# A recurrence's rounds taken out of hardware loops, with constant semaphore waits in place of register waits

## The chip, the cores and the metric

The kernel runs on one core of a Trainium2 chip. The core has a matrix engine (TensorE, PE in the profile, its weight loads as PEld), VectorE (DVE), ScalarE (ACT), GpSimd (POOL) and SyncE (SP), which here only issues DMAs. Each engine works through its own list of instructions in order; they meet only in semaphores. The metric is the device time of one execution in microseconds, as the median of several runs.

## The reference, cut to what matters

`x` is 4 x 32 x 128 x 128 in fp32. A layer norm and a Fourier attention block are added to it, and the result, seen as 4 sequences of 4096 tokens of 128 channels, goes through a layer norm, a linear map with batch statistics, and a recurrence over the 4096 tokens, whose states are added to it:

```python
x = x + _L0_conv_ref(_ln_c(x), ...)
t = _to_tokens(x)
t = t + _L0_ffn_ref(_ln_t(t), L0_ffn_W, L0_ffn_V, L0_ffn_gamma, L0_ffn_beta)
...
    def step(yt, wx_t):
        yt = jax.nn.sigmoid(wx_t + yt @ Vt)
        return (yt, yt)
    y0 = jnp.zeros((B, H), dtype=Wx.dtype)
    _, ys = jax.lax.scan(step, y0, jnp.swapaxes(Wx, 0, 1))
```

`wx_t` is the normalized linear map of token t, `Vt` a 128 x 128 matrix.

## The kernel before

Up to about 520 us the kernel computes the attention block and the linear map; nothing of that is touched. The recurrence then is not run token by token. Each sequence is cut into 256 chunks of `STEPS` = 16 tokens, and all chunks advance together: one operation handles one step of the 256 chunks of one sequence, as a tile of 128 channels x 256. The four sequences are the `GR` = 4 groups.

A first sweep runs only the last 8 steps (`BURN`) of every chunk, from a guessed state. Its end states are handed to the next chunks as their starts, by `starts`, on VectorE: two copies for each group (L1385, of 128 x 224, and L1386, of 128 x 31). A second sweep then runs all 16 steps. `judge` compares the new end states with those that were used as starts. If they differ by more than `TOL`, a flag makes every engine repeat whole sweeps in a loop under `e.If`; in the profiled execution the flag is zero and no repeat is run.

A round is one step of all four groups. For each group it takes three operations on three engines: TensorE multiplies the state with `v_t` into PSUM (L588, called from `sweep` at L851 and L856; one such fp32 product is two weight loads and two matmul passes in the trace), VectorE adds the linear map's value to it (L1364, `add_z`), ScalarE takes the sigmoid and writes the new state (L990, L996), which is the input of the group's next product. The semaphores are `vy` (product done), `vy_wx` (addition done) and `state` (state written). Every engine has a `sweep` of its own; `recur` calls it on each.

In each `sweep` the first two rounds are written out, and their waits are on constants. The rest are turns of a loop (`Fori`, L852, L992, L1372), two rounds to a turn: 3 turns in the first sweep, 7 in the second. In a turn the wait's value depends on the loop's register `i`. Such a wait becomes an instruction of its own ahead of the operation; in the trace it stands as FUSED_REGOPS on the engine's sequencer (DVEq, ACTq, PEldq).

Beside this, GpSimd works on something that the recurrence does not need before `judge`: 32 additions of 128 x 512 (L581, fp32, two inputs in SBUF, `x1_g0`), one right behind the other. After the sweeps come the reading of the flag, 128 transposes on TensorE, 32 additions on VectorE (L1412) and 32 output DMAs.

Of the kernel before, what the change touches and what calls it, by code (L numbers as in the profile page):

```python
# [56 lines left out]
STEPS, BURN = 16, 8  # L57
# [78 lines left out]
def metaformer(nc, t, out):  # L136
# [4 lines left out]
    with ctx:  # L141
# [3 lines left out]
        def sem(name):  # L145
            return ctx.enter_context(nc.semaphore(name))
# [146 lines left out]
        def s(name):  # L293

            if name not in scn:
                scn[name] = len(scn)
                assert len(scn) <= 54
            return sc[:, scn[name]:scn[name] + 1]
# [16 lines left out]
        def S(name):  # L315

            if name not in sems:
                sems[name] = sem(name)
            return sems[name]
# [74 lines left out]
        def at(states, g, j):  # L394

            return states[:, :, bass.ds(j, 1), TB * g:TB * g + TB]

        def start(g):
            return start_a[:, :, TB * g:TB * g + TB].unsqueeze(2)

        def sums(g, dj):
            return PS[:, g + GR * dj, 0:Q * TB].rearrange("d (q j t) -> d q j t", q=Q, t=TB)

        def recur(e, sweep, starts=None, judge=None):


            sweep(0, 0, STEPS - BURN)
            if starts:
                starts(BURN)
            sweep(1, BURN, 0)  # L410
            rounds = BURN + STEPS
            if judge:
                judge(rounds)
            e.wait_ge(S("judged"), 1)
            again = e.value_load(FLAG[0:1, 0:1], min_val=0, max_val=1)
            with e.If(again > 0):
                with e.Fori(0, CHUNKS - 1) as i:
                    if starts:
                        starts(i * STEPS + rounds)
                    sweep(i + 2, i * STEPS + rounds, 0)  # L420
                e.wait_ge(S("state"), GR * (rounds + STEPS * (CHUNKS - 1)))
            e.wait_ge(S("state"), GR * rounds)

# [162 lines left out]
        def _(pe):  # L586
            def mm(o, l, rhs, start=True, stop=True, **k):
                return pe.matmul(o, l, rhs, start=start, stop=stop, **k)  # L588
# [144 lines left out]
            for g in range(32):  # L733
# [8 lines left out]
                if g >= 24:  # L742
                    n = g - 24
# [21 lines left out]
            for turn in range(0, G4 + LAG_P2, 4):  # L765
# [4 lines left out]
                for g in range(max(turn - LAG_P2, 0), min(turn - LAG_P2 + 4, G4)):  # L770
                    n, j = 4 * g // P2_T, 4 * g % P2_T
# [10 lines left out]
            for k, (bk, a) in X1_AT.items():  # L782
                n = 68 if 0 < k < 16 else 34
# [56 lines left out]
            pe.wait_ge(S("bn"), G4)  # L840
            mm(PS[:, 7, 511:512], v_t, ones[:, 0:1]).then_inc(S("v_sum_filled"), 1)

            def sweep(n, k0, j0):

                for dj in range(0 if j0 == 0 else 1, 2):
                    for g in range(GR):
                        if dj:
                            pe.wait_ge(S("state"), GR * k0 + g + 1)
                        else:
                            pe.wait_ge(S("start"), n * GR + (g + 1))  # L850
                        mm(sums(g, dj), v_t, at(y_s, g, j0) if dj else start(g)).then_inc(S("vy"), 1)  # L851
                with pe.Fori(1, (STEPS - j0) // 2) as i:  # L852
                    for dj in range(2):
                        for g in range(GR):
                            pe.wait_ge(S("state"), i * (2 * GR) + (GR * (k0 + dj) + g + 1 - GR))
                            mm(sums(g, dj), v_t, at(y_s, g, i * 2 + (j0 + dj - 1))).then_inc(S("vy"), 1)  # L856

            def judge(p):
                pe.wait_ge(S("gap"), 1)
                tr(PS[0:1, 0, 0:128], s("gap")).then_inc(S("gap_filled"), 1)  # L860

            recur(pe, sweep, None, judge)

            for g in range(G4):
# [9 lines left out]
        def _(act):  # L874
# [60 lines left out]
            for i in range(G4 + LAG_M2):  # L935
# [5 lines left out]
                if g >= 0 and (4 * g + 4) % P2_T == 0 or g == G4 - 1:  # L941
                    n = 4 * g // P2_T
# [36 lines left out]
            root(s("bs"), s("rt"))  # L979
            act.wait_ge(S("bn_ab"), 1)  # L980
            act.wait_ge(S("bn"), G4)
            def sweep(n, k0, j0):
                for dj in range(2):
                    for g in range(GR):
                        if j0 and dj == 0:
                            act.activation(at(y_s, g, j0), wx_step[:, g, :, j0:j0 + 1, :], ACT.Sigmoid,  # L986
                                           scale=s("bs"), bias=s("bb_guess")).then_inc(S("state"), 1)
                        else:
                            act.wait_ge(S("vy_wx"), GR * (k0 + dj - 1) + g + 1)
                            act.activation(at(y_s, g, j0 + dj), sums(g, dj), ACT.Sigmoid,  # L990
                                           bias=s("bb")).then_inc(S("state"), 1)
                with act.Fori(1, (STEPS - j0) // 2) as i:  # L992
                    for dj in range(2):
                        for g in range(GR):
                            act.wait_ge(S("vy_wx"), i * (2 * GR) + (GR * (k0 + dj - 1) + g + 1))
                            act.activation(at(y_s, g, i * 2 + (j0 + dj)), sums(g, dj),  # L996
                                           ACT.Sigmoid, bias=s("bb")).then_inc(S("state"), 1)

            recur(act, sweep)


        @block.vector
        def _(dve):
# [358 lines left out]
            def add_z(b, dj, j):  # L1362

                STT(sums(b, dj), wx_step[:, b, :, bass.ds(j, 1), :], s("bs"), sums(b, dj),  # L1364
                    ALU.mult, ALU.add).then_inc(S("vy_wx"), 1)

            def sweep(n, k0, j0):
                for dj in range(0 if j0 == 0 else 1, 2):
                    for g in range(GR):
                        dve.wait_ge(S("vy"), GR * (k0 + dj - 1) + g + 1)  # L1370
                        add_z(g, dj, j0 + dj)
                with dve.Fori(1, (STEPS - j0) // 2) as i:  # L1372
                    for dj in range(2):
                        for g in range(GR):
                            dve.wait_ge(S("vy"), i * (2 * GR) + (GR * (k0 + dj - 1) + g + 1))
                            add_z(g, dj, i * 2 + (j0 + dj))

            def starts(k):


                for g in range(GR):
                    dve.wait_ge(S("state"), k * GR + (g + 1 - GR))
                    a, b = TB * g, TB * g + TB
                    last = y_s[:, :, STEPS - 1, a:b]
                    dve.tensor_copy(start_a[:, 1:Q, a:b], last[:, 0:Q - 1, :])  # L1385
                    dve.tensor_copy(start_a[:, 0, a + 1:b], last[:, Q - 1, 0:TB - 1]).then_inc(S("start"), 1)  # L1386

            def judge(k):
# [16 lines left out]
                TS(FLAG[0:1, 0:1], sc[0:1, 63:64], -1.0, 1.0, ALU.mult, ALU.add).then_inc(S("judged"), 1)  # L1405

            recur(dve, sweep, starts, judge)
            for g in range(G4):
                dve.wait_ge(S("yt_filled"), g + 1)
# [30 lines left out]
```

## Time and profile before

| what | us |
|---|---|
| median of 3 runs | 619.43 |
| lowest and highest of them | 617.39, 620.93 |
| profiled execution, its own time | 622.1 |
| span of its profile | 620.3 |
| granted TensorE clock, mean over the span | 0.843 |
| from the first sweep's first product (525.77) to the second's (545.09) | 19.3 |
| from there to the second sweep's last burst of additions (578.70) | 33.6 |
| busy over the whole span: PE, DVE, ACT, POOL | 444.6, 423.5, 241.7, 259.6 |

Times in the rows are microseconds from the start of the span. "Idle before" in brackets is how long the engine had stood idle, and what ended that. A granted clock of 1.00 is 2.4 GHz on TensorE, 0.50 is 1.2 GHz. Ends of matmuls are modelled, and the spans of GpSimd are rough.

### The profile page before, as it was taken

Reading aid. Unit: us, or ns where it says so; the run is one execution under the profiler, and the core shown is the slowest. Engines: PE = TensorE matmul, PEld = TensorE weight load, DVE = VectorE, ACT = ScalarE, POOL = GpSimd, SP = SyncE. Lnnn points to the kernel's source line nnn. Section 1 sums busy time; section 2 is a strip of 40 time slices with the busy share of each in tenths; the row PEclk is TensorE's granted clock in tenths of the full one; section 3 lists DMA queues with packets and bytes.
Section 4 is the critical chain, followed back from the end, with each engine's and each line's share of the span. In section 5 each row is a group of like instructions: output and inputs, shape, how many; then the busy total and the mean of one; then the engine's idle time right before and its main releaser. Section 6 shows DMA issues by size and latency. Waiting matters only on the chain.

```text
span 620.3 us, 7899 instructions
## 1 busy us (share of the span) xinstructions
PE 444.6 (72%) x2517; PEld 356.2 (57%) x2517; DVE 423.5 (68%) x1065; ACT 241.7 (39%) x485; POOL 259.6 (42%) x264
## 2 busy tenths in 40 slices
PE   0687999999734467999889940846655654989591
PEld 0677999996500117999878940834332321656391
DVE  5899366731889886012499969477888755788792
ACT  1465310101110103332455501236888896768300
POOL 0534810000567710000898793667557609910000
PEclk9999965555956877999989975868999998889796
DMA  8820000032500001000004551000000000000099
GB/s 352 272 57 2 1 5 0 1 89 48 131 6 0 0 2 51 1 0 1 1 2 119 171 156 48 2 1 0 2 0 2 1 0 1 1 0 0 2 274 269
DMA packets 40341, 32.04 MB, mean 52 GB/s; under 512 B 4640, under 2 KB 37840, under 8 KB 39280
## 3 DMA queue, kind: packets, MB, share of 16 engines
q1 hardware_dynamic: 40304, 31.57, 17.2%
q8 instruction: 20, 0.33, 0.2%
q14 instruction: 17, 0.14, 0.1%
HBM read 21.01 MB, written 8.45 MB: 47 GB/s over the span
## 4 chain that ended last, share of the span: by engine, by line
PE 46%; DVE 36%; POOL 5%; ACT 5%; issue 4%; DMA 1%; DVEq 0%; SPq 0%; ACTq 0%
PE PS L588 43%; DVE SML L1035 6%; DVE BIG L1151 4%; PE PS L592 4%; POOL BIG L574 3%; DVE BIG L1332 3%; DVE BIG L1170 2%; POOL BIG L569 2%; DVE BIG L1412 2%; DVE SML L1346 2%; DVE BIG L364 1%; ACT BIG L894 1%; DVE BIG L1249 1%; DVE BIG L1245 1%; DVE BIG L1341 1%
## 5 line engine op out<-in xcount | busy, mean ns | idle before, releaser
L588 PE MATMUL PS<-CST,BIG 128*128 128x65 f32 (+6 forms) x1026 | 159.6, 359 | 8.5 <-DVE BIG L1332 3.3
L588 PEld LDWEIGHTS PS<-CST,BIG 128*128 128x128 f32 (+1 forms) x1026 | 146.1, 232 | 25.5 <-issue 13.7
L592 PE MATMUL PS<-CST,BIG 128*128 128x128 f32 (+2 forms) x460 | 76.6, 309 | 103.7 <-ACT SML L364 28.1
L592 PEld LDWEIGHTS PS<-CST,BIG 128*128 128x128 f32 (+2 forms) x460 | 62.0, 182 | 129.6 <-issue 79.1
L588 PE MATMUL PS<-BIG 128*128 128x128 f32 (+2 forms) x466 | 68.3, 458 | 27.9 <-DVE BIG L1151 14.6
L364 DVE COPY BIG<-PS 128x512 f32<-128x512 f32 (+2 forms) x49 | 32.7, 675 | 71.3 <-PE PS L592 38.4
L588 PEld LDWEIGHTS PS<-BIG 128*128 128x128 f32 (+2 forms) x466 | 45.2, 181 | 46.1 <-issue 16.9
L364 ACT ACTIVATE BIG<-PS 128x512 f32<-128x512 f32 (+5 forms) x53 | 29.9, 564 | 104.8 <-PE PS L588 71.0
L553 POOL TENSOR_TENSOR BIG<-BIG,SML 128x512 f32<-128x512 f32 x32 | 32.0, 1037 | 77.2 <-ACT BIG L931 77.2
L1035 DVE BATCH_NORM_STATS2 SML<-BIG 128x6 f32<-128x128 f32 x256 | 53.4, 277 | 7.4 <-DMA BIG<-in_x 6.3
L588 PE MATMUL PS<-SML,BIG 128*128 128x128 f32 x256 | 57.7, 387 | 0.5 <-DVE SML L1204 0.5
L588 PEld LDWEIGHTS PS<-SML,BIG 128*128 128x128 f32 x256 | 56.9, 312 | 0.7 <-DVE SML L1204 0.7
L588 PE MATMUL PS<-BIG,SML 128*128 (+3 forms) x182 | 48.8, 416 | 7.7 <-ACT BIG L986 5.8
L569 POOL TENSOR_TENSOR BIG<-BIG,SML 128x512 f32<-128x512 f32 x32 | 33.2, 1037 | 45.6 <-DVE SML L1057 30.5
L1364 DVE SCALAR_TENSOR_TENSOR PS<-BIG,SML,PS 128x256 f32<-128x256 f32 x92 | 41.3, 490 | 11.8 <-PE PS L588 11.7
L965 ACT ACTIVATE BIG<-BIG,SML 128x128 f32<-128x128 f32 x112 | 46.1, 482 | 4.4 <-DVE SML L1057 4.4
L588 PEld LDWEIGHTS PS<-BIG,SML 128*128 128x128 f32 x182 | 32.8, 202 | 22.8 <-issue 10.2
L559 POOL TENSOR_TENSOR BIG<-BIG 128x512 f32<-128x512 f32 x32 | 42.9, 1359 | 6.2 <-DMA BIG<-in_x 5.7
L574 POOL TENSOR_TENSOR BIG<-BIG 128x512 f32<-128x512 f32 x32 | 40.5, 1268 | 0.0
L588 PE MATMUL PS<-SML 128*128 128x512 f32 (+1 forms) x72 | 37.6, 615 | 2.8 <-DVE SML L1386 2.2
L581 POOL TENSOR_TENSOR BIG<-BIG,SML 128x512 f32<-128x512 f32 x32 | 31.9, 1042 | 17.5 <-ACT BIG L965 17.5
L493 POOL TENSOR_SCALAR BIG<-BIG,SML 128x128 f32<-128x128 f32 x48 | 21.7, 464 | 41.5 <-DVE SML L1057 41.5
(210 smaller groups left out, 592.9 us busy)
## 6 DMA issues: line engine op xcount, KB each, us to landing
BIG<-in_x SPq DMA_DIRECT2D x8, 1024.0 KB, 12.1
BIG<-in_x SPq DMA_DIRECT2D x32, 256.0 KB, 2.9
out_x<-BIG SPq DMA_DIRECT2D x32, 256.0 KB, 3.6
BIG<-wy_rows SPq DMA_DIRECT2D x16, 128.0 KB, 3.5
BIG<-SML SPq DMA_DIRECT2D x16, 128.0 KB, 2.4
BIG<-in_L_conv_mixer_w SPq DMA_DIRECT2D x2, 544.0 KB, 6.3
CST<-in_const SPq DMA_DIRECT2D x1, 644.0 KB, 20.9
BIG<-in_L_conv_proj_w SPq DMA_DIRECT2D x1, 68.0 KB, 6.3
```

Of the source, the lines that this page charges most:

```text
L364: return e.activation(o, i, ACT.Copy) if e is scalar_engine else e.tensor_copy(o, i)
L553: pool.tensor_tensor(m1[:, v, :], a0[:, v, :], kap[:, v].unsqueeze(2).to_broadcast([128, 4, W]), ALU.mult).then_inc(S("ka0"), 1)
L559: pool.tensor_tensor(v, v, stage[:, g % 3, :, :], ALU.add).then_inc(S("xa"), 1)
L569: pool.tensor_tensor(m1[:, v, :], m1[:, v, :], bet[:, v].unsqueeze(2).to_broadcast([128, 4, W]), ALU.mult).then_inc(S("bm1"), 1)
L574: pool.tensor_tensor(a0[:, v, :], a0[:, v, :], m1[:, v, :], ALU.add).then_inc(S("xm"), 1)
L581: pool.tensor_tensor(a0[:, v, :], a0[:, v, :], g0[:, v].unsqueeze(2).to_broadcast([128, 4, W]), ALU.add).then_inc(S("x1_g0"), 1)
L588: return pe.matmul(o, l, rhs, start=start, stop=stop, **k)
L592: return pe.matmul(o, i, ident[0:n, 0:n], is_transpose=True, start=True, stop=True)
L965: last = act.activation(m1[:, n, :], a0[:, n, :], ACT.Identity, scale=ln_r[:, n:n + 1], bias=ln_b[:, n:n + 1])
L1035: last = dve.bn_stats(ln_st[:, c % 2, row, :], src[:, XR * c + row, :])
L1151: TT(prod(4 * hg + b)[:, 0, :, 0:n], xrep[:, b, :, 0:n], wr[:, hg, :, 0:1, :].to_broadcast([128, MW, n, MH]), ALU.mult).then_inc(S("prod_d ...
L1364: STT(sums(b, dj), wx_step[:, b, :, bass.ds(j, 1), :], s("bs"), sums(b, dj), ALU.mult, ALU.add).then_inc(S("vy_wx"), 1)
```

## The change

`recur` hands `sweep` a function that runs the turns. For the two sweeps that always run it is `unrolled`, a Python loop, so that the turns are written out and every wait is on a constant. For the sweeps that are repeated under `e.If` it is `looped`, the `Fori` of before.

```diff
+        def unrolled(n, turn):
+
+            for i in range(1, n):
+                turn(i)
+
         def recur(e, sweep, starts=None, judge=None):
+            def looped(n, turn):
+                with e.Fori(1, n) as i:
+                    turn(i)
...
-            sweep(0, 0, STEPS - BURN)
+            sweep(0, 0, STEPS - BURN, unrolled)
             if starts:
                 starts(BURN)
-            sweep(1, BURN, 0)
+            sweep(1, BURN, 0, unrolled)
...
-                    sweep(i + 2, i * STEPS + rounds, 0)
+                    sweep(i + 2, i * STEPS + rounds, 0, looped)
...
-            def sweep(n, k0, j0):
+            def sweep(n, k0, j0, turns):
...
-                with act.Fori(1, (STEPS - j0) // 2) as i:
+
+                def turn(i):
                     for dj in range(2):
                         for g in range(GR):
                             act.wait_ge(S("vy_wx"), i * (2 * GR) + (GR * (k0 + dj - 1) + g + 1))
                             act.activation(at(y_s, g, i * 2 + (j0 + dj)), sums(g, dj),
                                            ACT.Sigmoid, bias=s("bb")).then_inc(S("state"), 1)
+
+                turns((STEPS - j0) // 2, turn)
```

The `sweep` of TensorE and that of VectorE are changed in the same way.

VectorE's list before, from the end of the first sweep's written-out additions to the first rounds of its loop and on to the copies (ISA is the wait on a register's value; L1364 is the addition, L1385 and L1386 are the copies of `starts`):

```order
611 L1364 SCALAR_TENSOR_TENSOR PS<-BIG,SML,PS 128x256 [waits vy] x3
612 L1372 UNCONDITIONAL_BRANCH
613 L1372 ISA
614 L1364 ISA [waits vy]
615 L1364 SCALAR_TENSOR_TENSOR PS<-BIG,SML,PS 128x256
616 L1375 REGISTER_ALU
...
636 L1372 REGISTER_ALU
637 L1372 COMPARE_AND_BRANCH
638 L1385 COPY SML<-BIG 128x7x32 [waits state]
639 L1386 COPY SML<-BIG 128x31
```

The same place now (L1380 is the addition, L1404 and L1405 are the copies):

```order
610 L1380 SCALAR_TENSOR_TENSOR PS<-BIG,SML,PS 128x256 [waits vy,bn_ab]
611 L1380 SCALAR_TENSOR_TENSOR PS<-BIG,SML,PS 128x256 [waits vy] x27
612 L1404 COPY SML<-BIG 128x7x32 [waits state]
613 L1405 COPY SML<-BIG 128x31
...
620 L1380 SCALAR_TENSOR_TENSOR PS<-BIG,SML,PS 128x256 [waits vy] x64
```

The wait has moved into the addition itself, and register additions and branches are gone; the order of additions and copies is the same.

TensorE's list before, at the start of the first sweep's loop:

```order
530 L588 MATMUL PS<-BIG,SML 128x256 [waits state] x4
531 L852 UNCONDITIONAL_BRANCH
532 L852 ISA
533 L588 ISA [waits state]
534 L588 MATMUL PS<-BIG,SML 128x256
535 L855 REGISTER_ALU
```

TensorE's list now, from there to the end of the second sweep and the reading of the flag (L425; L598 is the product):

```order
530 L598 MATMUL PS<-BIG,SML 128x256 [waits state] x28
531 L598 MATMUL PS<-SML 128x256 [waits start] x4
532 L598 MATMUL PS<-BIG,SML 128x256 [waits state] x60
533 L602 MATMUL PS<-CST,SML 1x128 [waits gap]
534 L425 TENSOR_LOAD FLAG [waits judged]
```

Each product carries its wait; the 28 + 4 + 60 products are those that ran before, in their order. ScalarE's list changes likewise.

## Rows read from the trace of the kernel before

**Rows 1.** The page, chain that ended last: shares of the span by engine.

```profile
PE 46%; DVE 36%; POOL 5%; ACT 5%; issue 4%; DMA 1%; DVEq 0%; SPq 0%; ACTq 0%
```

**Rows 2.** Busy time by stretch of the recurrence (x: instructions).

```profile
core 0: us, PE busy (x) PEld busy (x) DVE busy (x) ACT busy (x) POOL busy (x), PEclk, DMA share, GB/s
525.70:531.80 6.10, 6.03 (x14) 4.86 (x15) 2.83 (x6) 3.86 (x9) 6.10 (x7) 0.50 0.00 0
...
543.70:548.90 5.20, 3.81 (x10) 3.07 (x11) 3.96 (x12) 1.85 (x4) 1.11 (x2) 0.67 0.00 0
548.90:581.10 32.20, 29.35 (x120) 19.46 (x118) 27.32 (x65) 26.54 (x61) 0.00 (x0) 1.00 0.00 0
```

**Rows 3.** Chain that ended last, in order of time: start, us, engine, tile, line.

```profile
543.44 1.51 DVE SML L1385
...
552.50 1.99 PE PS L588 x8
554.63 1.99 PE PS L588 x8
```

**Rows 4.** Timeline of VectorE: start, us, engine, line, operation, count [idle before].

```profile
535.36 1.88 DVE L1364 SCALAR_TENSOR_TENSOR PS<-BIG,SML,PS 128x256 f32<-128x256 f32 x4 [0.19 <-PE PS L588]
...
541.77 1.77 DVE L1364 SCALAR_TENSOR_TENSOR PS<-BIG,SML,PS 128x256 f32<-128x256 f32 x4 [0.39 <-PE PS L588]
...
549.24 1.78 DVE L1364 SCALAR_TENSOR_TENSOR PS<-BIG,SML,PS 128x256 f32<-128x256 f32 x4 [0.17 <-PE PS L588]
551.26 1.77 DVE L1364 SCALAR_TENSOR_TENSOR PS<-BIG,SML,PS 128x256 f32<-128x256 f32 x4 [0.23 <-PE PS L588]
...
578.70 1.77 DVE L1364 SCALAR_TENSOR_TENSOR PS<-BIG,SML,PS 128x256 f32<-128x256 f32 x4 [0.33 <-PE PS L588]
```

**Rows 5.** Three lines' register waits: sequencer, ns min/median/max, first and last start.

```profile
L1364 DVEq FUSED_REGOPS  x80: 57/57/100, 530.4 to 579.9; - x80
...
L996 ACTq FUSED_REGOPS  x80: 46/46/80, 531.1 to 580.5; - x80
...
L588 PEldq FUSED_REGOPS  x56: 46/46/69, 550.3 to 579.0; - x56
```

**Rows 6.** Timeline, narrow windows: one looped round of group 0, step by step.

```profile
552.50 0.69 PE L588 MATMUL PS<-BIG,SML 128*128 x2
...
553.36 0.49 DVE L1364 SCALAR_TENSOR_TENSOR PS<-BIG,SML,PS 128x256 f32<-128x256 f32 x1 [0.33 <-PE PS L588]
...
553.99 0.47 ACT L996 ACTIVATE BIG<-PS,SML 128x256 f32 x1 [0.36 <-DVE PS L1364]
...
554.62 0.19 PEld L588 LDWEIGHTS PS<-BIG,SML 128*128 128x128 f32 x1 [0.53 <-issue]
```

**Rows 7.** Timeline, narrow windows: the second sweep's start, with constant waits.

```profile
544.88 0.16 DVE L1386 COPY SML<-BIG 128x31 f32<-128x31 f32 x1
...
545.09 0.89 PE L588 MATMUL PS<-SML 128*128 128x256 f32 x2 [2.19 <-DVE SML L1386]
...
546.02 0.49 DVE L1364 SCALAR_TENSOR_TENSOR PS<-BIG,SML,PS 128x256 f32<-128x256 f32 x1 [0.15 <-PE PS L588]
...
546.55 0.47 ACT L990 ACTIVATE BIG<-PS,SML 128x256 f32<-128x256 f32 x1 [2.42 <-DVE PS L1364]
```

**Rows 8.** Timeline and one line's durations: VectorE operations that meet GpSimd's.

```profile
542.77 2.04 POOL L581 TENSOR_TENSOR BIG<-BIG,SML 128x512 f32<-128x512 f32 x2
...
543.44 1.51 DVE L1385 COPY SML<-BIG 128x224 f32<-128x224 f32 x1
...
543.77 1.04 POOL L581 TENSOR_TENSOR BIG<-BIG,SML 128x512 f32<-128x512 f32 x1
...
L1385 DVE COPY SML<-BIG x4: 277/278/1515, 543.4 to 545.5; 128x224 f32<-128x224 f32 x4
...
483.92 1.27 POOL L574 TENSOR_TENSOR BIG<-BIG 128x512 f32<-128x512 f32 x1
...
484.50 0.77 DVE L1341 TENSOR_SCALAR BIG<-BIG,SML 128x128 f32<-128x128 f32 x1
```

## What I predicted, before the changed kernel ran

> **What bounds the kernel now.** I first read the chain that ended last by engine: TensorE 46%, VectorE 36% [rows 1]. An average over stages says little about an edit in one of them, so I next read the stretches of the recurrence [rows 2]. From 548.9 to 581.1 us TensorE runs at its full clock (granted 1.00, that is 2.4 GHz) and is busy 29.35 of 32.20 us, VectorE 27.32, ScalarE 26.54, GpSimd 0. Three engines are each some 85 to 90% busy and none is full: that is what a ring of dependent steps looks like, not a full engine. The chain in order of time says the same [rows 3]: it advances in pieces of TensorE work that restart some 2.1 us apart (552.50, then 554.63), and between two pieces TensorE does not set the pace.
>
> The ring is one round of one group: product on TensorE, the addition L1364 on VectorE, the sigmoid L996 on ScalarE, and the next round's product of the same group. Four groups follow one another through it. VectorE's four additions of a round come as one burst, and the bursts start at 551.26 and, 13 rounds later, at 578.70 [rows 4]: 27.44/13 = **2.11 us a round**. Within a burst, of constant waits and at the full clock, four additions take 1.78 us, so they follow at (1.78 - 0.49)/3 = 0.43 us [rows 4]. TensorE fed all four without waiting there, so four groups need 4 x 0.43 = 1.72 us of it. A round costs 2.11, not 1.72, because the first group has not come round yet.
>
> **The change, part by part.** It takes 80 of the 92 operations (96 on ScalarE) of each engine out of loops: 24 rounds in all, 20 of them looped. The order rows show what goes: in front of each operation the wait (an ISA row), mostly an addition on a register behind it, and two rows at each turn. Nothing is added on the path but straight code, and no operation passes another.
>
> *The register waits.* They last 57 ns on VectorE, 46 on ScalarE and 46 on TensorE's sequencer [rows 5], and the operation is dispatched only behind them. What counts is the whole hop. One looped round, step by step [rows 6]: TensorE 552.50 for 0.69, hop 0.17 to VectorE at 553.36, 0.49, hop 0.14 to ScalarE at 553.99, 0.47, hop 0.16 to TensorE's load at 554.62. Sum 2.12, the measured round. The same hops with a constant wait and an idle receiver [rows 7]: the products end at 545.09 + 0.89 = 545.98 and VectorE starts at 546.02, 0.04; it ends at 546.51 and ScalarE starts at 546.55, 0.04; a VectorE copy ends at 544.88 + 0.16 = 545.04 and TensorE, which waited for it, starts at 545.09, 0.05 (taken for the hop from ScalarE). New round: 0.69 + 0.04 + 0.49 + 0.04 + 0.47 + 0.05 = **1.78 us**, still above TensorE's 1.72, so latency stays the bound, narrowly. Saving 2.11 - 1.78 = 0.33. The bounds: 0.39, if TensorE's 1.72 is reached; below, 0.20, if only 57 + 46 + 46 = 149 ns and a little more of the hops go. I take 0.33, since all three hops are measured.
>
> *Second sweep.* 13 x 0.33 = 4.3 us, and 0.13 for VectorE's hop into the first of them: **4.4** (2.8 to 5.2). The first eight operations already have constant waits and run at the low clock, where TensorE is the bound.
>
> *Branches and register additions.* At nothing: they run beside the engines' work. A branch comes once in two rounds; the round from 552.50 to 554.63 takes 2.13 against the mean of 2.11, so hardly 0.04 a turn can hang on it.
>
> *First sweep.* Here six rounds are looped. The first of them runs at the low clock (granted 0.50, 1.2 GHz, up to 531.8 [rows 2]); TensorE is then busy 6.03 of 6.10 us with 14 passes, 0.43 a pass, two a product, so 4 x 2 x 0.43 = 3.44 us a round, and faster hops bring nothing. From 535.36 to 541.77 three rounds take 6.41 [rows 4]: 6.41 - 3 x 1.78 = 1.07, and the round and a half before them give some 0.5. VectorE would thus come to the end of the sweep **1.6 us sooner**, at 541.8 instead of 543.44.
>
> *What is late next there.* The copies L1385 and L1386, which hand each group's last state to the next chunk; TensorE cannot begin the second sweep without them. The first copy took 1.51 us where its three like took 0.28 [rows 8], and it stands on the chain with all of it [rows 3]. Beside it GpSimd ran its last two L581 back to back, 542.77 to 544.81, and the copy ended at 544.95, 0.14 after them. It had been waiting when the first of the two gave way to the second, which started at 543.77, and was not let in. GpSimd's stream of 32 does not depend on the recurrence, so it still ends at 544.81. Either the copy again waits it out, and the second sweep begins at 545.09 as now: gain 0. Or it slips in between two L581: L1341 at 484.50 ended at 485.27, 0.08 after the GpSimd instruction that it met, with another right behind [rows 8]. Then the copy of group 0 is done a microsecond or two sooner, but each of the eight copies meets another L581, and the last groups' copies are not sooner by more than some 0.3. I put that at 0.8 and its bounds at 0 and 1.1. I take **0**: the nearest row is that of the copy itself, in the same stream.
>
> The Trainium skill ("SBUF — State Buffer", section on who interferes with whom) says that VectorE in a two-port mode, which a copy can enter, and GpSimd exclude each other for a whole instruction, and that the second to issue waits until the first is finished. The stretched copy agrees in kind; taken literally, with one instruction as the longest wait, it would have ended 0.14 after 542.77 + 1.04, at 543.95, and the row's 544.95 differs. By the rule the second sweep starts sooner, which is the rival priced above at 0.8; by the row it does not.
>
> *Behind the second sweep* the check of the chunk ends, the reading of the flag and the output stay and move forward whole.
>
> **Sum**, against the profiled execution's own time: 622.1 - 4.4 - 0 = 617.7. That execution lies 2.7 above the median of 619.43, mostly by its being profiled; the saving carries over: 619.43 - 4.4 = **615.0**.
>
> **Rivals.**
> - *The copies slip in between* GpSimd's instructions. For it: L1341; against: the copy's own row. 4.4 + 0.8 = 5.2, so 614.2. The SBUF page of the Trainium skill, as told above, stands on this rival's side.
> - *The hops shrink less than they look.* The constant hops come from one group with an idle receiver at the low clock. If part of the 0.33 lies in waking an engine or in the groups' spacing, and a round ends at 1.95, 13 x 0.16 = 2.1 remain: 617.3, inside what a measurement can tell from no change.
> - *The change does nothing*: other waits stand in the place of those removed. The order rows show none; 619.4.
> - *The clock* (slower). While the copies wait, TensorE is idle: now for 2.19 us up to 545.09 [rows 7], after the change for 1.6 more, 3.8, and the clock already falls there (granted 0.67 on average from 543.7 to 548.9, [rows 2]). A round at the low clock costs 3.44 instead of 1.78, 1.66 more. A low stretch longer by 2.7 rounds, 9 us, eats the whole gain; by six rounds it gives 619.4 - 4.4 + 10.0 = 625.0. Against it: both sweeps of now reach the full clock soon, the first within 6.1 us of its start, the second 3.8 us after 545.09 (by 548.9, [rows 2]).
>
> **How the numbers follow.** Forecast 62%; copies slip in 16%; smaller hops 14%; nothing 4%; clock 4%. Under 0.5% (3.1 us) a measurement of this kernel can't tell a difference from none, so faster is 0.78 (the first two), same 0.18, slower 0.04. Range: from both gains at their bounds, 619.4 - 5.2 - 1.1, rounded to 613.0, to the low end of the hops at 617.4, which also takes in the runs' own spread of 617.39 to 620.93 around a median; it leaves out no change and the clock.
>
> **What would show it.** In the profile after: VectorE's bursts in the second sweep 1.78 apart, not 2.11; no register operations on the additions' line; a gap of 0.04 from addition to sigmoid; the first sweep's last burst some 1.6 us sooner; the first copy stretched to about 3 us and ended just after GpSimd's last L581, and the second sweep's first product where it was, 19 to 20 us after the first sweep's. I am wrong if the bursts stay above 1.9 (the hops), if that first product comes a microsecond sooner (the copies), or if the low clock lasts past the second sweep's second round.

## The result, and the profile after

| | before | after |
|---|---|---|
| median of 7 runs, us | 619.77 | 615.95 |
| lowest and highest | 617.39, 620.93 | 613.57, 617.76 |
| profiled execution, its own time | 622.1 | 617.17 |
| span of its profile | 620.3 | 615.4 |
| instructions | 7899 | 7362 |
| granted TensorE clock, mean | 0.843 | 0.843 |

The ratio (of the mean times) is **0.9941 (0.9916 to 0.9965)**: 3.7 us less, with an interval of 2.2 to 5.2; the two medians lie 3.8 apart. The forecast was 615.0, a ratio of 0.993, which is inside the interval. That the time fell is clear of the noise. That it fell by over 0.5%, as the forecast had it, is likely (0.59% was measured) but not shown by the times, since the interval begins at 0.35%.

First VectorE's timeline in the kernel after, over both sweeps. L1380 is the addition that was L1364, L1404 and L1405 are the copies that were L1385 and L1386.

```profile
531.52 9.86 DVE L1380 SCALAR_TENSOR_TENSOR PS<-BIG,SML,PS 128x256 f32<-128x256 f32 x22 [0.36 <-PE PS L598]
541.29 3.05 DVE L1404 COPY SML<-BIG 128x224 f32<-128x224 f32 x1
...
544.34 0.28 DVE L1404 COPY SML<-BIG 128x224 f32<-128x224 f32 x1
...
548.62 26.81 DVE L1380 SCALAR_TENSOR_TENSOR PS<-BIG,SML,PS 128x256 f32<-128x256 f32 x60 [0.32 <-PE PS L598]
```

The bursts of [rows 4] have become one row: 60 additions in 26.81 us with no idle time that splits them, where each four of before stood apart by 0.17 to 0.39. The first copy takes 3.05 us, twice the 1.51 of [rows 8].

The chain that ended last, in order of time, answers to [rows 3]:

```profile
541.38 2.96 DVE SML L1404
544.34 0.09 DVE SML L1405
...
544.47 4.13 PE PS L598 x10
...
548.62 1.78 DVE PS L1380 x4
...
550.41 1.78 DVE PS L1380 x4
```

Rounds are now 550.41 - 548.62 = 1.79 apart, and nothing but the additions stands between them. That VectorE carries 43% of the chain where it had 36% [rows 1] doesn't make it the bound by itself: the ring still goes through three engines, and where their gaps are this small this view keeps the chain on one of them. The windows, with the columns of [rows 2], show how close all of it now is:

```profile
543.70:548.90 5.20, 4.43 (x13) 3.62 (x14) 3.78 (x13) 1.90 (x4) 0.49 (x1) 0.67 0.00 0
548.90:577.00 28.10, 26.01 (x117) 17.19 (x115) 28.09 (x68) 26.60 (x60) 0.00 (x0) 1.00 0.00 1
```

From 548.9 on, VectorE is busy 28.09 of 28.10 us (27.32 of 32.20 before): its additions last 0.49 and follow one another every 0.43 to 0.49, so that no gap is left, and the next round's first addition starts where the last round's fourth ends. The round is (26.81 - 1.79)/14 = 1.787 us by the row of 60 additions, less the last round's four. Inside a round the additions follow at 0.433, so TensorE could feed a round in 4 x 0.433 = 1.73, 0.055 under that. Being busy all the time does not make VectorE the bound either: in the trace every addition of this stretch starts 0.04 behind the end of its own product, so none of them waits for VectorE.

**Where the 4.9 us of the two spans are.** From the first sweep's first product to the second's it was 525.77 to 545.09, 19.32 us, and is 525.14 to 544.47, 19.33. From there to the end of the last addition it was 35.38 and is 548.62 + 26.81 - 544.47 = 30.96: **4.42 less**. The final transposes begin at 581.97 instead of 587.01, 5.04 sooner; the 0.62 beyond 4.42 lie ahead of the recurrence, where nothing was changed. That start moves by some microseconds from one execution to the next (that product comes at 521.48 to 525.77 in the traces of this study), which is why the traces are compared from the first product on, and times only by medians.

### The profile page after: what moved, and what is told of

It is laid out like the page before. It is cut to its first block, busy times and chain, and to the rows that moved or that the text cites. A ratio compares the mean times of both kernels' runs of the same rounds, so it can differ in the third digit from the quotient of the medians.

```text
span 615.4 us, 7362 instructions
## 1 busy us (share of the span) xinstructions
PE 439.8 (71%) x2517; PEld 353.3 (57%) x2517; DVE 428.4 (70%) x1065; ACT 242.3 (39%) x485; POOL 259.9 (42%) x264
## 4 chain that ended last, share of the span: by engine, by line
DVE 43%; PE 41%; POOL 5%; ACT 5%; issue 4%; DMA 1%; DVEq 0%; SPq 0%
PE PS L598 37%; DVE SML L1051 6%; DVE PS L1380 6%; DVE BIG L1167 4%; PE PS L602 4%; POOL BIG L584 3%; DVE BIG L1186 3%; DVE BIG L1348 3%; POOL BIG L579 2%; DVE BIG L1431 2%; DVE SML L1362 2%; DVE BIG L364 1%; ACT BIG L907 1%; DVE BIG L1265 1%; DVE BIG L1261 1%
## 5 line engine op out<-in xcount | busy, mean ns | idle before, releaser
L598 PE MATMUL PS<-CST,BIG 128*128 128x65 f32 (+6 forms) x1026 | 157.8, 355 | 8.5 <-DVE BIG L1348 3.3
L598 PEld LDWEIGHTS PS<-CST,BIG 128*128 128x128 f32 (+1 forms) x1026 | 145.0, 230 | 24.9 <-issue 14.1
L598 PE MATMUL PS<-BIG 128*128 128x128 f32 (+2 forms) x466 | 68.7, 461 | 27.4 <-DVE BIG L1167 13.1
L598 PEld LDWEIGHTS PS<-BIG 128*128 128x128 f32 (+2 forms) x466 | 45.1, 181 | 45.7 <-issue 16.8
L598 PE MATMUL PS<-SML,BIG 128*128 128x128 f32 x256 | 57.8, 387 | 0.5 <-DVE SML L1220 0.5
L598 PEld LDWEIGHTS PS<-SML,BIG 128*128 128x128 f32 x256 | 56.9, 312 | 0.7 <-DVE SML L1220 0.7
L598 PE MATMUL PS<-BIG,SML 128*128 128x256 f32 (+2 forms) x182 | 45.2, 412 | 5.8 <-ACT BIG L999 5.8
L1380 DVE SCALAR_TENSOR_TENSOR PS<-BIG,SML,PS 128x256 f32<-128x256 f32 x92 | 41.5, 489 | 5.6 <-PE PS L598 5.5
L598 PEld LDWEIGHTS PS<-BIG,SML 128*128 128x128 f32 x182 | 30.8, 203 | 19.2 <-ACT BIG L999 5.9
L598 PE MATMUL PS<-SML 128*128 128x512 f32 (+1 forms) x72 | 37.5, 614 | 4.2 <-DVE SML L1405 3.6
```

## Experiments

All durations are measured from the first sweep's first product (P1) or the second sweep's (P2). The summary stands here, the reasons below; e1 to e4 shared one chip, e5 and e9 another, e6 and e8 a third.

| kernel | ratio to before | P1 to P2 | P2 to last addition's end | first copy |
|---|---|---|---|---|
| before | 1 | 19.32 | 35.38 | 1.51 |
| after | 0.9941 (0.9916 to 0.9965) | 19.33 | 30.96 | 3.05 |
| e1_first | 1.002 (0.9998 to 1.0041) | 19.33 | 35.22 | 3.45 |
| e2_second | 0.9929 (0.9903 to 0.9956) | 19.33 | 30.96 | 1.51 |
| e3_after_hold | 0.9867 (0.9834 to 0.9899) | 16.47 | 29.34 | 0.28 |
| e4_before_hold | 0.9976 (0.9953 to 0.9999) | 18.15 | 33.74 | 0.28 |
| e5_reduce | 0.988 (0.9851 to 0.9909) | 16.68 | 29.62 | 0.38 |
| e8_warm | 0.9917 (0.9901 to 0.9934) | 19.33 | 29.34 | 3.17 |
| e9_best | 0.9819 (0.979 to 0.9847) | 15.49 | 29.35 | 0.28 |
| e6_dve | one run | 19.33 | 33.53 | 2.41 |
| e6_act | one run | 19.34 | 34.01 | 1.94 |
| e6_pe | one run | 19.34 | 34.05 | 2.10 |

In each of the eight kernels that leave both GpSimd's stream and the copy as they are, P1 to P2 is 19.32 to 19.34, while the first copy takes anything from 1.51 to 3.45.

**Which sweep pays?** My theory: the second alone, since the first's gain is lost in the copy. The rival: both pay in part, and something else takes it back.

```diff
# e1_first
             sweep(0, 0, STEPS - BURN, unrolled)
...
-            sweep(1, BURN, 0, unrolled)
+            sweep(1, BURN, 0, looped)
```

> Only the first sweep's three turns are written out, the second sweep stays a loop. My theory: the first sweep ends 1.6 us sooner, the first copy of the end states then waits that much longer for GpSimd (about 3.05 us instead of 1.51), the second sweep's first product stays 19.3 us after the first sweep's first, and the time is that of before: 0.0 us, ratio 1.000. Rival (the first sweep's gain reaches the end): 1.6 us faster, ratio 0.997, first products 17.7 us apart.

```diff
# e2_second
-            sweep(0, 0, STEPS - BURN, unrolled)
+            sweep(0, 0, STEPS - BURN, looped)
...
             sweep(1, BURN, 0, unrolled)
```

> Only the second sweep's seven turns are written out, the first sweep stays a loop. My theory: the whole gain of the change, 4.4 us, ratio 0.993: rounds of 1.79 us in the second sweep, the first copy at 1.51 us as before, first products 19.3 us apart. Rival (both sweeps share the gain by their 6 and 14 looped rounds): 14/20 of 4.4, 3.1 us.

Medians are 620.14 and 615.03 beside 619.34. The first sweep written out alone shows no gain, the second alone gives all that the change gives (4.4 by the ratio and by the trace). The times of e2_second alone, 2.7 to 6.0 less, would still allow its rival's 3.1; the trace does not, with 30.96 behind P2 and everything before P2 as it was. VectorE and TensorE in e1_first:

```profile
537.23 3.45 DVE L1404 COPY SML<-BIG 128x224 f32<-128x224 f32 x1
521.48 15.31 PE L598 MATMUL PS<-BIG,SML 128*128 128x256 f32 x56 [5.80 <-ACT BIG L999]
540.81 3.53 PE L598 MATMUL PS<-SML 128*128 128x256 f32 x8 [4.02 <-DVE SML L1405]
```

The copy comes 537.23 - 521.48 = 15.75 us after P1, 1.9 sooner than before's 17.67, lasts 1.9 longer (3.45 against 1.51), and P2 is where it was. In the kernel after, where the first sweep is the same, it comes 16.15 us after P1. The 0.4 between the two goes with the clock: from 4 to 6 us behind P1 it was 0.65 here and 0.50 there, after the same idle time of 5.8 us.

**Is it GpSimd's stream that keeps the copy out?** If so, a hole in that stream at the copies frees them. The hold lets GpSimd do its first 27 of 32 operations, then wait until the second sweep's first round has written its states, which is behind the copies; the last five follow, and nobody waits for them soon. It went into the kernel after and, as a check that the same copy costs something without the change, into the kernel before.

```diff
# e3_after_hold (in the kernel after), e4_before_hold (in the kernel before)
             for g in range(G4):
+                if g == 27:
+                    pool.wait_ge(S("state"), GR * (BURN + 1))
```

> The changed kernel, and GpSimd's last five additions (27 to 31 of 32) wait until the second sweep's first round has written its states, so that none of them runs while VectorE copies. My theory (the copy is kept out by GpSimd's stream): all four first copies at 0.28 us, first products 16.6 us apart instead of 19.3, 2.7 us faster than the change alone, 7.1 faster than before, ratio 0.9885. Rival (the copy is slow for another reason, such as waiting for the last sigmoid or for data just written): the first copy stays at 3 us and the time at that of the change, ratio 0.994.

> The kernel before, with the same hold of GpSimd's last five additions. My theory: the first copy takes 0.28 instead of 1.51 us, 1.2 us faster than before, ratio 0.998, first products 18.1 us apart. With the hold, writing the turns out is then worth 7.1 - 1.2 = 5.9 us, against 4.4 without it. Rival (the first sweep's turns are worth nothing by themselves): the hold is worth as much here as in the changed kernel.

Medians are 611.08 and 617.67. In e3_after_hold, VectorE's, GpSimd's and TensorE's rows at the handover (the added lines move all by two):

```profile
541.23 0.28 DVE L1406 COPY SML<-BIG 128x224 f32<-128x224 f32 x1
...
512.28 26.96 POOL L593 TENSOR_TENSOR BIG<-BIG,SML 128x512 f32<-128x512 f32 x27 [17.49 <-ACT BIG L980]
...
541.65 1.99 PE L600 MATMUL PS<-SML 128*128 128x256 f32 x8 [0.86 <-DVE SML L1407]
```

GpSimd stands still from 539.24, the copy takes 0.28 and P2 comes 2.86 sooner than in the kernel after: the cause is shown. But the gain is larger than the copy. I had expected 2.7 over the change; by the trace it is 2.86 + (30.96 - 29.34) = 4.5, and the medians differ by 4.9 from 615.95 and 4.0 from e2's 615.03, which was on the same chip. In the kernel before the same: 19.32 - 18.15 = 1.17 from the copy, and 35.38 - 33.74 = 1.64 more behind P2. The time of e4, 1.7 less with an interval of 0.1 to 2.9, hardly tells this from nothing; the size is the trace's. With the hold in both, writing the turns out is worth (18.15 - 16.47) + (33.74 - 29.34) = 6.1 us by the traces (5.9 expected) and 6.6 by the medians, where it was 4.4 without: now the first sweep's 1.7 get through as well. Four microseconds from P2 on, as windows of after, of before and of e3_after_hold:

```profile
544.47:548.47 4.00, 4.00 (x11) 3.24 (x12) 2.74 (x10) 1.55 (x4) 0.00 (x0) 0.57 0.00 0
```

```profile
545.09:549.09 4.00, 4.00 (x11) 3.23 (x12) 2.74 (x10) 1.42 (x3) 0.00 (x0) 0.57 0.00 0
```

```profile
541.65:545.65 4.00, 4.00 (x18) 2.93 (x18) 3.99 (x14) 2.90 (x8) 0.90 (x1) 1.00 0.00 0
```

With the wait for the copy the clock granted is 0.57 and TensorE makes 11 passes; without it, 1.00 and 18.

**Is the clock a cost of its own?** e3 takes away the idle time and the low clock together. So the next kernel keeps the copy's wait and fills TensorE's idle time with seven products whose results nobody uses.

```diff
# e8_warm (in the kernel after)
+                if isinstance(n, int) and n == 1:
+                    for k in range(7):
+                        mm(PS[:, k % 4, 256:512], v_t, CST[:, 0:256])
```

> The changed kernel with seven idle products on TensorE (results unused, 0.43 us each) between the first sweep's last product and the wait for the copies, GpSimd as in the change. My theory (the second sweep's first rounds run at the low clock because TensorE idled for 3.3 us while the copy was kept out): first products still 19.3 us apart, but the granted clock stays at 1.00 after them and the second sweep is 1.6 us shorter (29.3 instead of 31.0 us from its first product to its last addition): 1.6 us faster than the change alone. Rival (the low clock follows from something else, or the hold of GpSimd shortened the second sweep in another way): 31.0 us as in the change.

TensorE's and VectorE's rows, and the window from P2 on:

```profile
538.99 3.19 PE L598 MATMUL PS<-CST,SML 128*128 128x256 f32 x14
542.89 1.99 PE L598 MATMUL PS<-SML 128*128 128x256 f32 x8 [0.72 <-DVE SML L1408]
...
539.59 3.17 DVE L1407 COPY SML<-BIG 128x224 f32<-128x224 f32 x1
```

```profile
542.89:546.89 4.00, 4.00 (x18) 2.93 (x18) 4.00 (x14) 2.72 (x7) 0.00 (x0) 1.00 0.00 0
```

P1 to P2 stays 19.33, with the copy at 3.17, and P2 to the last addition falls from 30.96 to 29.34, the very 1.62 of e3. So the low clock behind the wait is a cost of its own, 1.6 us, and hangs on TensorE's idle time. By the median (614.66 beside 619.77) the interval reaches from 4.1 to 6.1 less than before and meets that of the change, so it is the trace that shows this, not the time.

**Is a hole in the stream needed at all?** If the copy is refused for the kind of instruction that it is, another kind does the same work beside the full stream: a reduction over an axis of length one.

```diff
# e5_reduce (in the kernel after)
-                    dve.tensor_copy(start_a[:, 1:Q, a:b], last[:, 0:Q - 1, :])
-                    dve.tensor_copy(start_a[:, 0, a + 1:b], last[:, Q - 1, 0:TB - 1]).then_inc(S("start"), 1)
+                    dve.tensor_reduce(start_a[:, 1:Q, a:b], last[:, 0:Q - 1, :].unsqueeze(3), AX.X, ALU.max)
+                    dve.tensor_reduce(start_a[:, 0, a + 1:b], last[:, Q - 1, 0:TB - 1].unsqueeze(2), AX.X,
+                                      ALU.max).then_inc(S("start"), 1)
```

> The changed kernel; VectorE moves the end states with a reduction over an axis of length one in place of a copy, same values, same engine, same place, and GpSimd's stream is not held. My theory (a copy is kept out by GpSimd because it uses a port that both share, and a reduction does not): the first one takes about 0.4 us in the middle of GpSimd's stream, the second sweep starts 2.5 us sooner (first products 16.8 us apart), and the clock does not fall: about 4 us faster than the change alone, ratio to before 0.988. Rival (any VectorE operation on these tiles waits for GpSimd's stream): 3 us as the copy, ratio 0.994.

VectorE's, GpSimd's and TensorE's rows:

```profile
540.05 0.38 DVE L1404 TENSOR_REDUCE SML<-BIG 128x224 f32<-128x224 f32 x1
...
537.91 5.03 POOL L591 TENSOR_TENSOR BIG<-BIG,SML 128x512 f32<-128x512 f32 x5
...
540.58 1.99 PE L598 MATMUL PS<-SML 128*128 128x256 f32 x8 [0.96 <-DVE SML L1405]
```

GpSimd runs without a gap from 537.91 to 542.94, right across the reduction of 540.05, which takes 0.38. Median 611.37 beside 619.82. P1 to P2 is 0.21 longer than in e3_after_hold and the stretch behind P2 0.28. Of these 0.49 us 0.10 lie in the first sweep (16.15 against 16.05 from P1 to the first of these operations). The rest is the reductions' own: VectorE takes 1.55 us from the first of them to its next addition (540.05 to 541.60), and with the copies of e3_after_hold 1.15 (541.23 to 542.38).

**Are the three hops what was summed?** Each engine alone gets constant waits; the others keep the loop.

```diff
# e6_dve (e6_act: nc.scalar, e6_pe: nc.tensor)
+            mine = unrolled if e is nc.vector else looped
-            sweep(0, 0, STEPS - BURN, unrolled)
+            sweep(0, 0, STEPS - BURN, mine)
...
-            sweep(1, BURN, 0, unrolled)
+            sweep(1, BURN, 0, mine)
```

> Constant waits on VectorE alone, loops on TensorE and ScalarE. My theory (each hop is shortened by itself, and a round is the sum of its steps): the hop to VectorE shrinks from 0.17 to 0.04, the second sweep's rounds take 2.11 - 0.12 = 1.99 us. Rival (the rounds are set by one engine's loop, and the gain comes only when all three are written out): 2.11 us.

> Constant waits on ScalarE alone. My theory: the hop to ScalarE shrinks from 0.14 to 0.04, rounds of 2.01 us. Rival: 2.11 us.

> Constant waits on TensorE alone. My theory: the hop to TensorE shrinks from 0.14 to 0.04 or 0.05, rounds of 2.01 to 2.02 us; the three savings of the three kernels add up to the change's 2.11 - 1.79 = 0.32. Rival: 2.11 us.

VectorE's bursts, the last of the second sweep and one some rounds before it, in e6_dve, e6_act and e6_pe:

```profile
556.59 1.78 DVE L1381 SCALAR_TENSOR_TENSOR PS<-BIG,SML,PS 128x256 f32<-128x256 f32 x4 [0.22 <-PE PS L599]
...
574.44 1.78 DVE L1381 SCALAR_TENSOR_TENSOR PS<-BIG,SML,PS 128x256 f32<-128x256 f32 x4 [0.19 <-PE PS L599]
```

```profile
556.89 1.77 DVE L1381 SCALAR_TENSOR_TENSOR PS<-BIG,SML,PS 128x256 f32<-128x256 f32 x4 [0.25 <-PE PS L599]
...
574.93 1.77 DVE L1381 SCALAR_TENSOR_TENSOR PS<-BIG,SML,PS 128x256 f32<-128x256 f32 x4 [0.23 <-PE PS L599]
```

```profile
553.11 1.77 DVE L1381 SCALAR_TENSOR_TENSOR PS<-BIG,SML,PS 128x256 f32<-128x256 f32 x4 [0.25 <-PE PS L599]
...
577.31 1.77 DVE L1381 SCALAR_TENSOR_TENSOR PS<-BIG,SML,PS 128x256 f32<-128x256 f32 x4 [0.25 <-PE PS L599]
```

Nine rounds take 17.85 and 18.04 us, twelve take 24.20: 1.98, 2.00 and 2.02 a round. Against 2.11 that is 0.13 on VectorE, 0.11 on ScalarE and 0.09 on TensorE, 0.33 together, and the change saved 2.111 - 1.787 = 0.32. The savings add up, as a ring of latencies has it; an engine that were the bound would give all or nothing. The stretches behind P2 say the same: 1.85, 1.37 and 1.33 less than before, 4.55 together, against the change's 4.42. These three have one time each (617.87, 618.40, 620.95), and the last is even above the 619.77 of before; a single time says less than the rounds.

**Both findings together, and the hold put twice.** Ahead of the recurrence VectorE works on single columns beside the same stream of GpSimd's. In the kernel after, three of these:

```profile
521.58 0.68 DVE L1046 TENSOR_TENSOR SML<-SML 128x1 f32<-128x1 f32 x1
522.30 0.97 DVE L1372 TENSOR_TENSOR SML<-SML 128x1 f32<-128x1 f32 x1
523.30 0.96 DVE L1373 TENSOR_TENSOR SML<-SML 128x1 f32<-128x1 f32 x1
```

And the one of GpSimd's additions that runs beside the third:

```profile
523.20 1.04 POOL L591 TENSOR_TENSOR BIG<-BIG,SML 128x512 f32<-128x512 f32 x1
```

It ends at 523.20 + 1.04 = 524.24, and the column operation beside it at 523.30 + 0.96 = 524.26. The two ahead of it end in the same way, 0.01 to 0.02 behind the end of a GpSimd addition. So these operations wait for the one addition under way and get in, where the copy was kept out to the end of the stream.

The last experiment holds GpSimd there as well, until these are done:

```diff
# e9_best (in the kernel after)
             for g in range(G4):
+                if g == 6:
+                    pool.wait_ge(S("bn_ab"), 1)
+                if g == 20:
+                    pool.wait_ge(S("state"), GR * (BURN + 1))
```

> The changed kernel with GpSimd's stream kept out of both places where VectorE needs the shared path: its additions from number 6 on wait until the recurrence's factors are ready, those from number 20 on until the second sweep's first round is done. My theory: in the small operations ahead of the recurrence (TENSOR_TENSOR of 128 x 1 at 0.68, 0.96 and 0.96 us where the same line takes 0.16 elsewhere) 2.1 us go, the rest as with the hold alone: 2.1 us faster than that kernel, about 609 us, ratio 0.983. Rival (GpSimd's stream, ending some 7 us later, becomes the last thing that the check of the chunk ends waits for): no faster than with the hold alone, 0.987.

VectorE's rows in e9_best, and TensorE's at P1 and P2:

```profile
519.79 0.16 DVE L1050 TENSOR_TENSOR SML<-SML 128x1 f32<-128x1 f32 x1
519.99 0.16 DVE L1376 TENSOR_TENSOR SML<-SML 128x1 f32<-128x1 f32 x1
...
536.60 0.28 DVE L1408 COPY SML<-BIG 128x224 f32<-128x224 f32 x1
...
521.53 14.63 PE L602 MATMUL PS<-BIG,SML 128*128 128x256 f32 x56 [3.97 <-ACT BIG L1003]
537.02 1.99 PE L602 MATMUL PS<-SML 128*128 128x256 f32 x8 [0.86 <-DVE SML L1409]
```

Median 607.87 beside 619.82, the fastest kernel here. From the first of these column operations to P1 it is 1.74 us (3.56 in the kernel after). P1 to P2 is 15.49, 1.0 less than in e3_after_hold although the copies are alike. That is the clock: over the first 4 us from P1 it is 0.50 in all these kernels, but not over the next two. In the kernel after, in e1_first and in e9_best:

```profile
529.14:531.14 2.00, 2.00 (x6) 1.64 (x5) 1.27 (x3) 0.95 (x2) 2.00 (x3) 0.50 0.01 4
```

```profile
525.48:527.48 2.00, 2.00 (x8) 1.65 (x7) 1.27 (x4) 0.95 (x2) 2.00 (x3) 0.65 0.01 4
```

```profile
525.53:527.53 2.00, 2.00 (x10) 1.54 (x9) 1.87 (x5) 1.52 (x4) 2.00 (x3) 0.99 0.01 4
```

TensorE had been idle 3.97 us ahead of P1 in e9_best, and 5.8 in the other two. That the shorter idle time brought the whole of this 1.0 us is not shown: in e1_first the clock rose earlier than in the kernel after at the same idle time, and the copy came 0.4 sooner. Over the hold alone e9_best gains 1.8 ahead of P1 and 1.0 behind it, 2.8 by the traces, where 2.1 were expected; the clock's part had not been foreseen.

## Why the prediction was right, point by point

- **What bounds the kernel: a ring of latencies.** Right. The three hops each save their own share (e6), and the round ends 0.055 above what TensorE needs. In the trace of the kernel after, one lap of one group, from the load's start, is 0.70 + 0.04 + 0.49 + 0.03 + 0.47 + 0.05 = 1.78 to 1.79 us, for every group and round between 551 and 561 us: that is the whole round, with no time spent waiting for an engine. The 0.055 is all that is left before TensorE would be the bound; no run pressed the ring further.
- **The hops.** Forecast 0.04, 0.04 and 0.05, a round of 1.78 and a saving of 0.33; measured 1.79 and 0.32. In the kernel after, narrow windows of the timeline:

```profile
560.40 0.19 PEld L598 LDWEIGHTS PS<-BIG,SML 128*128 128x128 f32 x1 [0.19 <-ACT BIG L1010]
...
560.45 0.65 PE L598 MATMUL PS<-BIG,SML 128*128 128x256 f32 x2
560.65 0.49 DVE L1380 SCALAR_TENSOR_TENSOR PS<-BIG,SML,PS 128x256 f32<-128x256 f32 x1
560.74 0.47 ACT L1010 ACTIVATE BIG<-PS,SML 128x256 f32<-128x256 f32 x1
...
561.14 0.49 DVE L1380 SCALAR_TENSOR_TENSOR PS<-BIG,SML,PS 128x256 f32<-128x256 f32 x1
561.17 0.47 ACT L1010 ACTIVATE BIG<-PS,SML 128x256 f32<-128x256 f32 x1
561.26 0.19 PEld L598 LDWEIGHTS PS<-BIG,SML 128*128 128x128 f32 x1
```

  The load starts at 560.40 and its product ends at 561.10, 0.70 later. The product ends at 561.10 and the addition starts at 561.14; an addition ends at 561.14 and a sigmoid starts at 561.17; a sigmoid ends at 561.21 and a load starts at 561.26. That is 0.04, 0.03 and 0.05, in the full stream as at the idle start of [rows 7]. The hops fell by more than the register wait's row lasts at its median: by 0.13 on VectorE where that is 57 ns, and by 0.11 and 0.09 on the others where it is 46 [rows 5]. Taking the whole hop and not that row was the choice that made the number right; by the rows alone the round would have been 1.96.

  Where the rest was, the chain of the kernel before shows, for a hop to ScalarE and one to VectorE (ACTq and DVEq are the waits on a register):

```profile
540.15 0.07 ACTq L996
540.23 0.05 issue
540.28 0.48 ACT BIG L996
...
542.94 0.06 DVEq L1364
543.00 0.05 issue
543.04 0.06 DVE PS L1364
```

  Behind the wait's row come another 0.05 us until the operation starts, and these go too when the wait is part of the operation. And on a round's first group, which sets the pace, the wait's row lasts longer than its median: in the round of [rows 6] 0.075 us on VectorE, 0.060 on ScalarE and 0.069 on TensorE.
- **Second sweep, 4.4.** Measured 4.42. One detail was off: of the first eight operations, which have constant waits before as after, only four run at the low clock; the burst at 549.24 [rows 4] lies in the stretch of 1.00 [rows 2]. It changes nothing in the sum. The upper end of the range, 617.4, is not what the sum's own lower bound of 2.8 gives, which is 616.6.
- **Branches and register additions, nothing.** Nearly right. Each kernel of e6 takes one engine's out with its waits, so no run prices them alone, but the trace of before does. A register addition starts behind the start of its operation and lasts 0.03 to 0.04 us beside it. The turns themselves do show: every second round, TensorE's hop on the first group is 0.157 instead of 0.134, and the bursts come 2.124 apart instead of 2.100 (they start at 551.262, 553.362, 555.486, 557.586). A turn is two rounds, so it seems to cost some 0.02 us, under 0.2 in the second sweep. It was inside the mean round of 2.11 from which the saving was taken, so the sum had it without naming it.
- **First sweep, 1.6 sooner.** Measured 541.29 - 525.14 = 16.15 us from P1 to the copy against 17.67, so 1.5 sooner.
- **The copy waits GpSimd's stream out, gain 0.** Right, and to the hundredth of a microsecond (19.32 and 19.33). GpSimd's timeline in the kernel after, its last four additions:

```profile
540.16 4.04 POOL L591 TENSOR_TENSOR BIG<-BIG,SML 128x512 f32<-128x512 f32 x4
```

  The four last operations start at 540.16 and a microsecond apart each, and the stream ends at 544.20; the copy, queued at 541.29, ends at 544.34, 0.14 after it, as in [rows 8]. It let two of them start ahead of it, some 542.2 and 543.2; in e1_first, three. The rule of the Trainium skill ("SBUF — State Buffer", section on who interferes with whom), read as a wait of one instruction at the most, would have let it end near 542.3. That the copy does not run beside GpSimd's instructions the traces confirm; that one instruction is the longest wait they contradict: 1.51, 3.05 and 3.45 us, each to the end of the stream. Why L1341 of [rows 8] got in and this copy did not, no run shows. Here the row was the better guide than the rule, and the rival "slip in" (614.2) did not come.
- **The clock.** As a rival it did not come: 0.57 over the 4 us from P2 on, before and after, though TensorE was idle 3.62 us instead of 2.19 (and 0.61 in e1_first after 4.02). What the prediction lacked is that the low clock behind the copy was there to be won. It counted the first rounds of the second sweep as given; e3, e5 and e8 show that they cost 1.6 us, and that they do so because of the copy's wait. It touches no term of the sum, but it is why e3 gained 4.5 and not the 2.7 that I expected with the same reasoning.
- **The sum against the median.** 4.4 was forecast, 3.7 measured, with 2.2 to 5.2 as the interval; e2_second, the same saving in another set of runs, came out at 4.4. The difference is within what the measurement can tell. That the execution of 622.1 lay above its median "mostly by its being profiled" is not borne out: the profiled execution lies 1.2 above the median of the kernel after and 2.5 below that of e1_first. Why it was slow, no run shows; the forecast does not need it, since the saving was taken from the median.

## What to carry to other kernels

Where small operations pass work round a ring of engines, add up one round from the trace, hop by hop, and price each hop from a place where the same hop has a constant wait: a wait on a register cost about twice what its own row shows at the median. When a stretch gets faster, look at what its end meets; here 1.5 us vanished in a copy that could not get past another engine's stream, and a hold of one line in that stream, or another instruction for the copy, gave about as much again as the change. An idle gap on TensorE can cost more than its own length: here 2.2 to 4.0 us of it brought a low clock behind them that cost another 1.6.

## What the runs showed of the hardware that I had not expected

- A VectorE copy of 128 x 224 fp32 was kept out by back-to-back GpSimd TENSOR_TENSORs over several instruction boundaries, until the stream's end: 3.05 and 3.45 us for one that takes 0.28 undisturbed. A TENSOR_REDUCE of the same tile ran at 0.38 beside the same stream (e5), and the additions that read PSUM too at their usual 0.49 (487 to 491 ns over all 92). TENSOR_TENSOR of single columns from SBUF took 0.68 to 0.97 beside it, each to the end of one GpSimd instruction, and 0.16 with the stream held (e9).
- After 2.19 to 4.02 us of TensorE's idle time the clock was 0.57 to 0.61 in the 4 us that followed; after 0.72 to 0.96 us it was 1.00. That cost 1.62 us behind P2 with GpSimd's stream as it was (e8 against the kernel after), and 1.64 with the stream held (e4 against before).
- A semaphore wait against a register costs 0.13 us on VectorE, 0.11 on ScalarE and 0.09 on TensorE more of a round than one against a constant (e6). About half of that is the wait's own row; the rest is the 0.05 between that row's end and the operation's start, and a longer row where the wait is the one that sets the pace.
